# Clearing transfers issued by SyncE, and two written-out dense stages with the layernorm statistics inside, in a graph network of four layers on one core

## The reference, cut to what matters

```python
def _general_conv(x, src, dst, W_msg, b_msg, W_self, b_self, n_nodes):
    msg = x[src] @ W_msg + b_msg
    agg = jax.ops.segment_sum(msg, dst, num_segments=n_nodes)
    return agg + x @ W_self + b_self
# layer 2
h = _general_conv(x, src, dst, W1_msg, b1_msg, W1_self, b1_self, n)
h = jax.nn.leaky_relu(h, negative_slope=0.1)
out = _general_conv(h, src, dst, W2_msg, b2_msg, W2_self, b2_self, n)
# around it
h = jnp.maximum(_layernorm(x, axis=-1), 0.0)
x = x + _L2_gnn_ref(h, ...)
```

## Time and profile before

| | us |
|---|---|
| median of 3 runs | 10185.92 (10169.62 to 10193.13) |
| the profiled execution | 10172.71, its span 10170.6 |
| GpSimd busy | 6515.4 (64% of the span) |
| TensorE matmul busy | 5979.7 (59%) |
| VectorE busy | 4870.8 (48%) |
| ScalarE busy | 2036.9 (20%) |
| mean granted TensorE clock | 0.751 |

### The profile page before, as it was taken

One profiled execution on the slowest core, in us unless ns is written; L12 is line 12 of the kernel. 1 busy time (PEld: TensorE's weight loads), 2 busy tenths in 40 slices (PEclk: granted clock), 3 DMA queues, 4 the chain that ended last, 5 costly groups with the idle time before them and its releaser, 6 DMA issues. The chain is left out here.

```text
span 10170.6 us, 136884 instructions
## 1 busy us (share of the span) xinstructions
PE 5979.7 (59%) x24639; PEld 4757.3 (47%) x24640; DVE 4870.8 (48%) x14032; ACT 2036.9 (20%) x5514; POOL 6515.4 (64%) x9285
## 2 busy tenths in 40 slices
PE   4788885774666666645555344555455465455544
PEld 2677774553544444433334233444344344444443
DVE  6455556776644444445556333334333342455555
ACT  2111111783322222210000100001000031223324
POOL 3777772000058888888888688884888816777750
PEclk9788887997877777766667677777777765667767
DMA  4555555663067777764444333332333325677764
GB/s 151 169 173 178 171 176 195 200 199 108 2 105 105 105 105 104 105 112 135 140 139 130 120 89 90 88 90 80 89 89 89 90 83 158 223 231 241 249 201 158
DMA packets 863543, 1389.54 MB, mean 137 GB/s; under 512 B 114551, under 2 KB 516805, under 8 KB 862997
## 3 DMA queue, kind: packets, MB, share of 16 engines
q0 software_dynamic: 315328, 634.04, 27.7%
q1 hardware_dynamic: 366180, 501.57, 15.2%
q10 hardware_dynamic: 181488, 248.03, 7.3%
HBM read 955.84 MB, written 427.35 MB: 136 GB/s over the span
## 5 line engine op out<-in xcount | busy, mean ns | idle before, releaser
L1030 POOL DMA_INDIRECT regionB<-table,gather_rows x3136 | 3105.2, 990 | 1007.2 <-POOLq L1032 606.5
L1771 POOL DMA_INDIRECT scatter_sums<-regionC,idx x880 | 1388.3, 1578 | 306.2 <-issue 246.6
L1136 PE MATMUL ps_p<-regionB,hot 128*128 x3520 | 1039.8, 458 | 768.3 <-DVE regionC L1197 576.8
L1136 PEld LDWEIGHTS ps_p<-regionB,hot 128*128 128x128 f32 x3520 | 815.6, 235 | 977.1 <-issue 833.9
L1033 POOL MEMSET regionA<- 128x192 f32 x3920 | 1124.8, 287 | 5.8 <-remote 1.6
L1136 PE MATMUL ps_p<-regionC,hot 128*128 x1760 | 646.2, 511 | 554.4 <-issue 433.3
L1030 POOL DMA_INDIRECT regionC<-table,gather_rows x784 | 755.2, 963 | 156.6 <-issue 99.3
L2113 PE MATMUL ps_p<-regionA 128*128 128x264 f32 x1760 | 578.4, 497 | 417.9 <-PEq L2108 191.7
L1136 PEld LDWEIGHTS ps_p<-regionC,hot 128*128 128x128 f32 x1760 | 440.4, 257 | 760.1 <-issue 691.4
L1844 PE MATMUL psC<-regionC 128*128 128x128 f32 x1760 | 371.2, 377 | 647.0 <-PEq L1842 644.6
L1203 DVE TENSOR_TENSOR regionA<-ps_own,own_bias 128x256 f32<-128x256 f32 x98 | 41.6, 425 | 1371.0 <-DVEq L1202 1014.9
(11 more groups left out here) (366 smaller groups left out, 10280.1 us busy)
## 6 DMA issues: line engine op xcount, KB each, us to landing
regionA<-edge_rows SPq DMA_DIRECT2D x440, 256.0 KB, 3.3
regionA<-edge_rows ACTq DMA_DIRECT2D x440, 256.0 KB
edge_rows<-regionB SPq DMA_DIRECT2D x196, 512.0 KB
edge_rows<-regionB SPq DMA_DIRECT2D x392, 256.0 KB
regionC<-srcrow_d SPq DMA_DIRECT2D x220, 256.0 KB
scatter_sums<-zero_rows ACTq DMA_DIRECT2D x8, 6400.0 KB, 41.5
regionB<-table,gather_rows POOLq DMA_INDIRECT x3136
regionA<-scatter_sums ACTq DMA_DIRECT2D x49, 1024.0 KB
```

Source lines behind the costliest of these rows:

```text
L1030: g.indirect_dma_start(out=rows_of(b * per + j), out_offset=None, in_=table, in_offset=bass.IndirectOffsetOnAxis(ap=idx[:, column:column + ...
L1136: x = te.matmul(ps[(u.c * VG + j) % NB], hot[:, b, 2 * j + k, :], at_tile(G, slot[j] * 2 + k), start=k == 0, stop=k == 1)
L1771: g.indirect_dma_start(out=scat, out_offset=bass.IndirectOffsetOnAxis(ap=idx[:, b, j:j + 1], axis=0), in_=sums[:, b, j, :], in_offset=None ...
```

## The change

It has three parts.

1. In `dense_loop` the call `beside` moves from ScalarE's list to SyncE's, behind the loads and ahead of the stores. So the three clearing transfers of the first dense phase are issued by SyncE. The five in the softmax stay with ScalarE.
2. `plain_pass` loads a second bias row (b_msg) and `own_out` adds `deg * b_msg` right away, by a second VectorE operation that waits for the first.
3. The two dense phases of layer 2 become `conv_dense`, written out on all engines. TensorE transposes `regionC` directly, without ScalarE's copy, and begins with two transposes before the weights are there. ScalarE only copies transposes. There are three buffers for them and four PSUM banks for results. VectorE's steps for a tile are staggered over neighbouring tiles. In the second one SyncE loads the weights first and then issues `bring_back`; the statistics (`bn_stats`) stand in the same phase, the stores to `x_kept` too, and `ln_stats` keeps only its short operations.

```diff
@@ dense_loop
                         sp.sem_inc(aux_full[1], 1)
+                        if beside:
+                            beside(sp)
                         if save:
...
                         a.sem_inc(aux_full[1], -1)
-                        if beside:
-                            beside(a)
@@ plain_pass
                             load(sp, W[:, :, :], kchunks(t[own[1]]))
-                            load(sp, ownb[:, :], bcast_row(t[own[2]]))
+                            load(sp, ownb[:, 0, :], bcast_row(t[own[2]]))
+                            load(sp, ownb[:, 1, :], bcast_row(t[own[3]]))
...
-                                v.tensor_tensor(at_tile(own[0], u.val // 2), psW[:, 0:D], ownb[:, :], ALU.add)
+                                y = at_tile(own[0], u.val // 2)
+                                v.tensor_tensor(y, psW[:, 0:D], ownb[:, 0, :], ALU.add).then_inc(own_v, 1)
+                                v.wait_ge(own_v, 1)
+                                v.sem_inc(own_v, -1)
+                                v.scalar_tensor_tensor(out=y, in0=ownb[:, 1, :], scalar=deg[:, bass.ds(u.val // 2, 1)], in1=y, op0=ALU.mult, op1=ALU.add)
@@ the dense phases of layer 2 (dense_loop with post_conv1 and post_conv2 goes)
+        def conv_dense(weights, sums, program, after):
+            DEEP = 4
...
+                    @block.sync
+                    def _(sp):
+                        load(sp, W[:, :, :], kchunks(t[weights]))
+                        loaded(sp)
+                        sp.sem_inc(aux_full[0], 1)
+                        after(sp, DEEP)
...
+                        for i in range(NT):
+                            if i >= 3:
+                                a.wait_ge(s_units.sem, i - 2 + s_units.base)
+                            a.wait_ge(tr_full[i % 2], 1)
+                            a.sem_inc(tr_full[i % 2], -1)
+                            a.activation(hT[:, i % 3].rearrange('p k n -> p (k n)'), psT[i % 2][:, 0:2 * P], ACT.Copy).then_inc(lhs_full[i % 2], 1)
...
+                        trans(0)
+                        trans(1)
+                        te.wait_ge(aux_full[0], 1)
+                        te.sem_inc(aux_full[0], -1)
+                        for i in range(NT):
+                            product(i)
+                            if i + 2 < NT:
+                                trans(i + 2)
...
+        def conv1(v, ps, deep):
...
+            for i in range(NT + 1):
+                if i < NT:
+                    total(i)
+                if i >= 1:
+                    leak(i - 1)
...
+                for i in range(NT + 2):
+                    if i < NT:
+                        total(i)
+                    if 1 <= i <= NT:
+                        residual(i - 1)
+                    if i >= 2:
+                        stats(i - 2)
+                v.drain()
...
+            def rows_conv2(sp, deep):
+                bring_back(sp)
+                for g in range(GT):
+                    sp.wait_ge(res_full[0], 1)
+                    sp.sem_inc(res_full[0], -1)
+                    sp.dma_start(x_d[g * GT * P:(g + 1) * GT * P, :].rearrange('(t p) c -> p t c', p=P), B256[:, g * GT:(g + 1) * GT, :]).then_inc(s_st.sem, 16)
...
-        ln_stats(B256, put_away)
+            ln_stats(B256, None, st2)
```

More of the change, by code:

```diff
@@ L429, in build, with ln_stats @@
             s_in.base = base_in + 32
-        def ln_stats(view, beside=None):
+        def ln_stats(view, beside=None, parts_of=None):
             with ExitStack() as ctx:
-                st = sb('ln_parts', [P, NT, 6], F32, ctx)
+                st = parts_of if parts_of is not None else sb('ln_parts', [P, NT, 6], F32, ctx)
                 with phase() as block:
@@ L1062, in plain_pass @@
                     W = sb('own_weights', [P, 2, D], F32, ctx)
-                    ownb = sb('own_bias', [P, D], F32, ctx)
+                    ownb = sb('own_bias', [P, 2, D], F32, ctx)
                     h_tile = sb('own_tile', [P, D], F32, ctx)
@@ L2614, in _ @@
                 sp.wait_ge(s_st.sem, s_st.base)
[L2615 to L2653, removed]
@@ new lines, in conv1, with total, leak @@
+        def conv1(v, ps, deep):
+            def total(i):
+                v.wait_ge(s_units.sem, i + 1 + s_units.base)
+                v.tensor_tensor(A256[:, i, :], A256[:, i, :], ps[i % deep], ALU.add).then_inc(own_v, 1)
+            def leak(i):
+                y = A256[:, i, :]
+                v.wait_ge(own_v, 1)
+                v.sem_inc(own_v, -1)
+                v.scalar_tensor_tensor(out=y, in0=y, scalar=0.1, in1=y, op0=ALU.mult, op1=ALU.max).then_inc(s_add.sem, 1)
+            for i in range(NT + 1):
[3 more added lines that the diff above has]
+                    leak(i - 1)
@@ new lines, in save_conv1 @@
+        def save_conv1(sp, deep):
+            for g in range(GT):
+                sp.wait_ge(s_add.sem, deep + (g + 1) * GT + s_add.base)
+                sp.dma_start(T3[g * GT * P:(g + 1) * GT * P, :].rearrange('(t p) c -> p t c', p=P), A256[:, g * GT:(g + 1) * GT, :]).then_inc(s_st.sem, 16)
+                s_st.base += 16
+            sp.wait_ge(s_st.sem, s_st.base)
+        conv_dense('L2_gnn_W1_msg', C256, conv1, save_conv1)
+        plain_pass('l2b', T3, B, C256, C[:, 0:NT * D], False, own=(A256, 'L2_gnn_W2_self', 'L2_gnn_b2_self', 'L2_gnn_b2_msg'))
@@ new lines, in build, with conv2, total, residual @@
+        with ExitStack() as ctx:
+            st2 = sb('conv_ln_parts', [P, NT, 6], F32, ctx)
+            def conv2(v, ps, deep):
+                def total(i):
+                    v.wait_ge(s_units.sem, i + 1 + s_units.base)
+                    v.tensor_tensor(A256[:, i, :], A256[:, i, :], ps[i % deep], ALU.add).then_inc(s_add.sem, 1)
+                def residual(i):
+                    v.wait_ge(s_add.sem, deep + i + 1 + s_add.base)
+                    if i % GT == 0:
+                        v.wait_ge(s_x[i // GT], 16)
+                    v.tensor_tensor(B256[:, i, :], B256[:, i, :], A256[:, i, :], ALU.add).then_inc(own_v, 1)
+                def stats(i):
+                    v.wait_ge(own_v, 1)
+                    v.sem_inc(own_v, -1)
+                    v.bn_stats(st2[:, i, :], B256[:, i, :])
+                    if i % GT == GT - 1:
+                        v.sem_inc(res_full[0], 1)
+                for i in range(NT + 2):
[5 more added lines that the diff above has]
+                        stats(i - 2)
+                v.drain()
+            def rows_conv2(sp, deep):
+                bring_back(sp)
+                for g in range(GT):
+                    sp.wait_ge(res_full[0], 1)
+                    sp.sem_inc(res_full[0], -1)
+                    sp.dma_start(x_d[g * GT * P:(g + 1) * GT * P, :].rearrange('(t p) c -> p t c', p=P), B256[:, g * GT:(g + 1) * GT, :]).then_inc(s_st.sem, 16)
+                    s_st.base += 16
+            conv_dense('L2_gnn_W2_msg', C256, conv2, rows_conv2)
+            ln_stats(B256, None, st2)
```

36 lines of the change are left out of this document (32 added, 4 removed).

## The result

The changed kernel takes 10042.48 us (median of 4 runs, 10027.30 to 10055.37) against 10182.51 (4 runs, 10169.62 to 10193.13) before: ratio 0.9862, 95% interval 0.9846 to 0.9878, 140 us faster. The forecast was 10072, range 10045 to 10110. The direction is right; the time lies 2.5 us under the range. The profiled execution took 10037.53 us, span 10035.4.

The account below looks back on a forecast made before the run. GpSimd's back-to-back fetches bound most of the kernel, and the change shortens three stretches without them. 34.6 + 27.0 + 53.0 - 0.8 - 5.5 = 108.3 us off a base of 10180.3 gives 10072, range 10045 to 10110.

Parts of the forecast that it names:

- Clearing, 34.6: First dense phase: ScalarE loses the issue of clearing transfers ahead of its first tile, 34.6 us, all on the path.
- the earlier of the two times I gave: First dense phase: SyncE's first store gets out at 146, or near 170 if it waits for the cleared bytes.
- First dense phase of layer 2, 27.0: Earlier first product and a 1.15 us step, with 2 us for the clock, save 27.0 us.
- The saturated bound, 1.08: Layer 2 dense phases: TensorE saturated, two transposes and a 256-column product, 1.08 us a tile; would give 30.4 and 56.4.
- layer 1's 1.40: Other bound for the layer 2 step: layer 1's dense phase, same product, light VectorE, 1.40 us; would give 15.0 and 41.0.
- Second one, 53.0: Second dense phase of layer 2 and statistics: weights first, statistics inside, shorter step; complete at 8274.1, 53.0 us saved.
- The two pieces that I took from rows, 18.7 and 16.3: Second dense phase of layer 2: 18.7 us from the earlier start, 16.3 from the statistics that stood alone.
- Bias row and bias step, -6.3 together: Plain passes: second bias row's load costs 0.8 us, the 98 new bias operations slow GpSimd's fetches by 5.5.
- the exclusion of the Trainium skill: Plain passes: two-SBUF-input VectorE operations and GpSimd SBUF reads exclude each other; if fetches count, the bias step term is -47.
- the step did not stay at a chain: Rival, layer 2 dense phases: step stays at layer 1's 1.40 us, twice 12 us lost, 10096; chance 0.12.
- the return of x: Rival, second dense phase of layer 2: weights or instructions wait behind 6 MB, 18.7 us lost, 10091; chance 0.08.
- the clearing and the bias step: Rivals: stores end first phase, 34.6 lost, 10107, chance 0.03; bias steps stop fetches 0.48 us each, 10113, chance 0.04.

Follow-up runs that it names:

- the bias-four kernel: Changed kernel with the bias step of the plain passes done four times in a row: 10052.78 us against 10161.54 before, ratio 0.9890.
- the two kernels that go beyond the change: Changed kernel with the remaining dense loops written out: 10042.23 us; the same with the score phase transposing H4 directly: 9999.91 us.

## Why the mechanism was right and two sizes of the sum were not

The step of the prediction that failed is the length that it gave the two dense phases of layer 2: a step of 1.15 us with 2.0 us for the clock on top. The runs showed 1.094 and under 1 us, and the two terms of 27.0 and 53.0 came to 32.7 and 59.6. Term by term:

- *Clearing, 34.6.* Right: 34.7 in the first comparison, 34.0 to 35.3 on the other chips. The stores ended nothing; the first got out at 147.95, 34.90 us behind the first clearing transfer's issue: the earlier of the two times I gave, without a wait for the cleared bytes.
- *First dense phase of layer 2, 27.0.* Mis-sized; it gave 32.7. Weights to first product 3.00 us, not 3.9, since ScalarE and the bias load were in the old path and the transposes run beside the load now; to the first addition 2.08, not 2.3; step 1.094, not 1.15 with 2.0 on top for the clock, 52.5 us in all where I had 57.2; last store 1.1 behind, not 1.0. In the windows the clock was 0.81 and 0.77, between the levels 1.2 and 2.4 GHz, over the first 8 us, of which 5 lie behind the first product. The first step is 1.66 long in place of 1.09 (second phase: 8139.32, 8140.98), and that is all the clock cost behind the first addition: under 1 us. The slow first product (2.04 us in place of 1.03) is already in the time to the first addition. So the 2.0 counted it twice, and a finer cut of rows 9 shows it: before, the clock was at its lower level (0.50) only up to about the first addition at 6941.4.

```profile
6937.00:6941.00 4.00, 2.97 (x9) 2.15 (x10) 0.00 (x0) 2.21 (x6) 0.00 (x0) 0.50 0.01 2
6941.00:6945.00 4.00, 2.94 (x15) 2.16 (x13) 2.42 (x6) 1.84 (x5) 0.00 (x0) 0.96 0.01 2
```

  The saturated bound, 1.08, was the right one to take. Of layer 1's 1.40 the loop held 0.15 (written out, layer 1's step is 60.0 / 48 = 1.25); ScalarE's tile copy, gone here too, was not tested alone.
- *Second one, 53.0.* Mis-sized the same way; it gave 59.6. The statistics were due at 66.65 us and complete at 59.7: 4.6 of that by the step and the clock, 1.1 by the start, and 1.2 by the tail of 2.0 us (8193.91 less 8191.9), where I had 3.2 with SyncE's issue and the change of phase, though the statistics wait for neither. The two pieces that I took from rows, 18.7 and 16.3, measured 19.8 and 17.5 when put back.
- *Bias row and bias step, -6.3 together.* Right in size: -7.8 on the second kind of chip (3.9 a pass), -4.3 in the first comparison. The load was undersized, 1.1 us a pass by the first fetch and not 0.4; the steps, 5.5 in the sum, are 2 x 2.6 = 5.2 on the second kind. On the first kind this isn't resolved: from first to last fetch it was 1155.5 and 1155.4 us before, 1154.3 and 1153.6 after, and the -4.3 came from the first load and from behind the last fetch. Nothing shows the exclusion of the Trainium skill (SBUF — State Buffer, "Who interferes with whom") between this operation and a fetch; the bias step keeps its 484 ns beside the fetches (L1209), and a fetch that meets it loses 0.04 to 0.07 us and not up to 0.48. The rows of L2398 beside GpSimd's arithmetic remain its only trace here.
- *Base and rest.* By the five touched stretches the change is worth 122.6 us in the first pair of traces, 118.6 in the second and 110.6 in the third (whose plain passes were the longest). By the medians of the same comparison the changed kernel gained 140.0, 115.7 and 108.7. The excess of the first lies in untouched phases and between the profiled execution and the median, for which the sum had no term. Of the 31.7 us by which the gain of 140.0 exceeds the forecast 108.3, 14.3 are in the touched stretches, 12.6 in untouched phases of the profiled execution and 4.8 in the medians. Windows over the fetch phase of layer 0 for before, the changed kernel and the bias-four kernel on chips of the first kind:

```profile
255.61:1640.06 1384.45, 1188.19 (x7040) 1068.39 (x7040) 686.14 (x1101) 261.93 (x440) 1032.82 (x1664) 0.83 0.54 170
```
```profile
222.60:1597.06 1374.46, 1176.39 (x7040) 1062.63 (x7040) 684.66 (x1101) 262.15 (x440) 1037.76 (x1664) 0.84 0.56 172
```
```profile
221.20:1603.20 1382.00, 1198.89 (x7040) 1081.32 (x7040) 686.24 (x1101) 261.60 (x440) 1043.33 (x1664) 0.82 0.54 171
```

The same instructions take 1374 to 1382 us, and 1371 to 1373 in the two kernels that go beyond the change: as wide a spread with the clearing on SyncE as the 10 us to the kernel before. The bias-four kernel, which has all parts of the change, gained 108.8 us in its comparison on a chip of this kind, though the interval of its ratio also admits 140. That the excess is variation is so supported, not proved, since there is no second trace of the kernel before on such a chip: its cause stays open. The range's low end was missed by the mis-sized 12 us and this together; either alone would have left the time inside.

None of the rivals came about: the step did not stay at a chain, and the return of x, the clearing and the bias step cost about what the sum said.

## What to carry to other kernels

When an edit takes everything but one engine out of a tile's chain, take that engine's saturated rate as the step, and use a looser row only if its own chain is still there. The issue of a bulk transfer can block the engine that issues it (35 us for three of 6400 KB here), so put it on the queue with slack behind it, and read that slack as the time from the last due instruction to the next phase. Before crediting or blaming a gain, sum it over the touched phases alone: 12.6 us of the 135.2 were elsewhere. Before adding a charge for a slow start, look whether the stretch that it covers is already counted.

## What was not expected of the hardware

- Chips differ: the same kernel takes 10182 us on one and 9761 on another. Of the 404 us between the spans, 345 are in the fetch phase of layer 0 (1384 to 1204) and the last attention (1689 to 1525), and 46 in the two plain passes; each dense phase agrees within 1.5 us. Window over the fetch phase, kernel before on the second kind:

```profile
257.80:1461.60 1203.80, 1084.41 (x7040) 1009.92 (x7040) 681.30 (x1101) 263.05 (x440) 1048.07 (x1664) 0.89 0.64 196
```

  The granted clock is 0.89 where it was 0.83, and the DMA moves 196 GB/s where it moved 170. Which of the two leads stays open.
- VectorE's operation on 128x256 starts 0.44 or 0.57 us behind the one that it needs, and 0.33 or 0.34 behind one that it doesn't need, at 0.40 to 0.43 us of duration.
- Three 6400 KB transfers block SyncE for 34.85 us and ScalarE for 34.52: the price goes with the transfers, not with the engine.
